# Attention with post-norm, then a 4-bit feed-forward, on one core: residual rows and next tokens loaded three slots sooner; at the seam between the two phases one weight load and two weight stores issued earlier

## The reference

```
qkv   = x @ w_qkv.T                      # 16 heads of 32
attn  = softmax(causal(q k.T / sqrt(32))) v
x1    = layernorm(x + attn @ w_o.T)
gate, up = x1 @ Wg.T, x1 @ Wu.T          # 512 -> 4096, weights as 4-bit codes
out   = layernorm(x1 + (gelu_tanh(gate) * up) @ Wd.T)
```

## Time and profile before

| what | value |
|---|---|
| unprofiled runs, median of 3 | 2737.24 us |
| profiled execution, its own time | 2741.44 us |
| its span, first to last instruction | 2739.6 us |
| TensorE busy | 2644.6 us, 97% of the span |
| VectorE, ScalarE, GpSimd busy | 57%, 40%, 30% |
| mean granted TensorE clock | 0.984 of full |
| moved by DMA | 493.5 MB, 180 GB/s on the mean |

### The profile page before, as it was taken

How to read it: one execution, slowest core, us unless ns; L and a number is a source line. 1 busy time by engine, 2 the same in 40 slices (tenths; PEclk the granted TensorE clock), 3 DMA queues, 4 the chain that set the end, 5 groups by cost and what they waited for, 6 DMA issues and landing times.

```text
span 2739.6 us, 37716 instructions
## 1 busy us (share of the span) xinstructions
PE 2644.6 (97%) x13314; PEld 2156.6 (79%) x13314; DVE 1552.0 (57%) x3224; ACT 1104.4 (40%) x2518; POOL 824.0 (30%) x992
## 2 busy tenths in 40 slices
PE   7999999999888999999999999999999999999998
PEld 6777777777566888888888888888888888888886
DVE  5677677767776888886433333543333364333334
ACT  4666665656543544443222222322222232222221
POOL 1444344434533443443211111321111132111112
PEclk9999999999889999999999999999999999999999
DMA  8676767676547565555554334355434435433441
GB/s 234 156 199 171 200 189 190 156 201 182 146 142 303 196 225 219 197 213 210 200 205 172 139 153 193 139 200 213 163 138 158 188 139 200 187 159 138 162 184 47
DMA packets 143085, 493.52 MB, mean 180 GB/s; under 512 B 11568, under 2 KB 48560, under 8 KB 118320
## 3 DMA queue, kind: packets, MB, share of 16 engines
q1 hardware_dynamic: 142896, 491.11, 52.3%
HBM read 356.84 MB, written 134.22 MB: 179 GB/s over the span
## 4 chain that ended last, share of the span: by engine, by line
PE 69%; DVE 2%; DMA 1%; issue 1%; POOL 0%; ACT 0%; SPq 0%; POOLq 0%; DVEq 0%; ACTq 0%
PE bank L1034 23%; PE bank L1036 23%; PE bank L1035 23%; DMA scale<-gate_scales 1%; PE bank L448 0%; PE bank L434 0%; DMA scale<-up_scales 0%; POOL probs L736 0%; DVE bstats L1482 0%; DVE acc L1425 0%; DMA x1T_scratch<-x_late 0%; DVE bits L1388 0%; PE bank L415 0%; SPq L915 0%; PE bank L458 0%
## 5 line engine op out<-in xcount | busy, mean ns | idle before, releaser
L1643 POOL TENSOR_TENSOR inter_l<-hid,inter_h 128x512 fp32r<-128x512 f32 x256 | 337.3, 1318 | 1375.5 <-ACT inter_h L1165 1375.5
L1425 DVE TENSOR_TENSOR acc<-acc,bank 128x512 f32<-128x512 f32 x512 | 350.0, 685 | 332.7 <-PE bank L1036 323.1
L1034 PE MATMUL bank<-wd,inter_h 128*128 128x512 f32 x1024 | 399.5, 390 | 10.7 <-DVE acc L1425 10.5
L1036 PE MATMUL bank<-wd,inter_l 128*128 128x512 f32 x1024 | 398.9, 390 | 0.0
L1035 PE MATMUL bank<-wd,inter_h 128*128 128x512 f32 x1024 | 398.9, 390 | 0.0
L736 POOL TENSOR_SCALAR probs<-probs,row_inv 128x128 f32<-128x128 f32 (+3 forms) x512 | 264.3, 538 | 363.4 <-DVE row_inv L657 363.4
L1444 DVE TENSOR_TENSOR hid<-hid,bank 128x512 f32<-128x512 f32 x192 | 131.9, 687 | 399.9 <-PE bank L1036 398.3
L1034 PE MATMUL bank<-bx_h,wg 128*128 128x512 f32 x896 | 350.4, 391 | 2.8 <-ACT bank L1165 2.8
L1035 PE MATMUL bank<-bx_l,wg 128*128 128x512 f32 x896 | 349.9, 390 | 0.0
L1036 PE MATMUL bank<-bx_h,wg 128*128 128x512 f32 x896 | 349.6, 390 | 0.0
L1034 PE MATMUL bank<-bx_h,wu 128*128 128x512 f32 x896 | 348.8, 389 | 0.0
(11 more groups left out here) (139 smaller groups left out, 4372.0 us busy)
## 6 DMA issues: line engine op xcount, KB each, us to landing
wg<-w_scratch SPq DMA_DIRECT2D x48, 1792.0 KB, 9.0
wu<-w_scratch SPq DMA_DIRECT2D x48, 1792.0 KB, 12.8
wd<-w_scratch SPq DMA_DIRECT2D x48, 1024.0 KB, 4.9
q_st<-qk_scratch SPq DMA_DIRECT2D x128, 256.0 KB, 5.1
k_st<-qk_scratch SPq DMA_DIRECT2D x128, 256.0 KB, 7.1
w_scratch<-wg SPq DMA_DIRECT2D x16, 1792.0 KB, 9.4
w_scratch<-wu SPq DMA_DIRECT2D x16, 1792.0 KB, 6.4
qk_scratch<-q_stage SPq DMA_DIRECT2D x32, 512.0 KB, 2.8
```

What stands on the lines that cost most here:

```text
L1034: pe.matmul(out, a(0), b(0), start=start, stop=False, skip_group_check=True)
L1036: return pe.matmul(out, a(1), b(0), start=False, stop=stop, skip_group_check=True)
L1425: dve.tensor_tensor(a, a, d_bank[n % 2][:, :], ALU.add).then_inc(d_added, 1)
L1643: pool.tensor_tensor(inter[1][:, m, t, :], hid[:, 2 * m + t, :], f32(inter[0][:, m, t, :]), ALU.subtract).then_inc(inter_split, 1)
```

## The change

In attention, chunks 0 and 1 of the next tokens are issued in slot 2 in place of slot 5. Chunks 2 and 3 stay in slots 6 and 7. The load of the residual rows is issued in slot 1 in place of slot 4; in the drain it stays in slot 0. In both places the load comes behind the slot's q or k write, and in slot 1 behind the stack read.

At the seam, SyncE issues the store of the up tile of round 0 at n = 25, and unit 7 and the store of the down tile at n = 30, which is ahead of the last two transposed tiles and ahead of the wait for attention's last stores. `rest` keeps the second load of `acc`. On VectorE `gate_up_low(1, 1)` moves from n = 28 to n = 29, and `down_low(0)` from n = 28 to n = 30, ahead of `unpack(5)`, which moves from n = 29 to n = 30.

```diff
@@ SyncE, attention @@
-                    if OUT_SLOT <= s + 1 < NEXT_SLOT and nxt:
-                        for c in (0, 1) if s + 1 == OUT_SLOT else (s + 2 - OUT_SLOT,) if s + 2 < NEXT_SLOT else ():
+                    if s in (2, OUT_SLOT, OUT_SLOT + 1) and nxt:
+                        for c in (0, 1) if s == 2 else (s + 2 - OUT_SLOT,):
                             load_x(b + 1, c)
...
-                    if s == (4 if cur else 0) and prev:
+                    if s == (1 if cur else 0) and prev:
@@ SyncE, feed-forward @@
             if n == 25:
                 load_unit(5)
                 store_w(0, 0)
+                store_w(0, 1)
...
+            if n == 30:
+                load_unit(7)
+                store_w(0, 2)
 
         def rest():
-            load_unit(7)
             load_acc(0, 1)
-            store_w(0, 1)
-            store_w(0, 2)
@@ VectorE, feed-forward @@
             if n == 28:
                 times_up(0, 1, 1)
+            if n == 29:
                 gate_up_low(1, 1)
+                times_up(0, 1, 0)
+            if n == 30:
                 down_low(0)
-            if n == 29:
-                times_up(0, 1, 0)
                 unpack(5)
```

## The result

The changed kernel took 2698.53 us (median of 4 runs, 2696.95 to 2699.56) against 2738.2 us for the kernel before (median of 4, 2732.85 to 2740.02). The ratio is 0.9858, 95% interval 0.9841 to 0.9875. The forecast was 2698, range 2687 to 2716. The profiled execution of the changed kernel spans 2695.2 us at a mean granted clock of 0.992, against 2739.6 us at 0.984.

A forecast was written before the change was run, and what follows sets the result against it. TensorE, busy 97% of the span, was taken to set the pace, so only idle or slow-clock time could be won. 27.8 + 4.5 + 7 = 39.3 us off 2737.24 gave 2698 us, range 2687 to 2716.

The forecast's parts named there:

- part 1: Attention, batches 0 to 6: next tokens issued in slot 2 remove the idle time of slot 6; 27.8 us.
- Part 2: Residual rows issued in slot 1, behind the k stack: delay to the stack 0 to 0.3 us, taken as none.
- Part 3: Batch 7: residual rows no longer queued ahead of the feed-forward's first tokens; 4.5 us, from 3 to 6.
- Part 4: Seam: 3.4 MB less ahead of unit 8, 7.9 us, less 1 us of delay; 7 us, bounds 3 to 15.
- It is worth little, since a later release holds TensorE anyway: Seam: removing TensorE's first idle time, 2.52 us before a late transposed tile, by VectorE's new order gains little.
- 3 us later in all: Seam: SyncE's last transposed tiles delayed 3 us, some 2.5 us from four issues, plus the down store ahead.
- Net 1 us later for the queue behind: Seam: the 3 us delay less some 2 us for unit 7's three issues leaves 1 us for later transfers.
- Units 9 and 10 are served by the same queue and move by the same time: Seam: units 9 and 10 land sooner by as much as unit 8, so 7 us was taken.
- A: Rival, slot 4 of batches 1 to 7: k stack lands late by sharing, 21 us back, 2719 us; chance 0.12.
- B: Rival: attention gains, the seam does not, through SyncE's later release or GpSimd's sums; 2705 us; chance 0.15.
- C: Rival: k stack lands only with residual rows and next tokens both, 6.9 us late; slower, 2745 us; chance 0.03.
- D: Rival: the change doesn't reach slot 6, another release lies close behind or slot 2's loads are late; about 2733 us; chance 0.04.

The follow-up runs named there:

- e1: Kernel before with only the next tokens' chunks 0 and 1 moved to slot 2; residual rows and seam as before: 2709.21 us, ratio 0.9898.
- e2: Kernel before with only the residual rows' load moved to slot 1; tokens stay in slot 5, seam as before: 2710.39 us, ratio 0.9904.
- e4: Changed kernel with the residual rows issued in slot 1 directly ahead of the k stack in place of directly behind it: 2720.72 us, ratio 0.9941.
- e5: Kernel before with only VectorE's new order at the seam; SyncE as before: 2734.42 us, ratio 0.9982.
- e9: Changed kernel with unit 7's load and the down tile's store put back behind the two late transposed tiles (n = 31): 2694.34 us, ratio 0.9841.
- e3: Kernel before with only the seam's edits of SyncE and VectorE; attention as before: 2734.58 us, ratio 0.9986.
- e7: Kernel before with only the up tile's store moved to n = 25; all else as before: 2732.87 us, ratio 0.9985.
- e8: Changed kernel with unit 8 loaded at n = 31, ahead of the final waits, and units 9 and 10 ahead of stores: 2693.6 us, ratio 0.9836.
- e10: As e9, with units 8, 9 and 10 each loaded ahead of the weight stores in their way in round 1: 2690.07 us, ratio 0.9826.

## Why the prediction was right, point by point

- **What bounds the kernel, and part 1.** Right. Forecast 27.8 us for batches 0 to 6, measured 28.5, batches 2 to 6 22.5 and 22.4. Pricing the stall by the period rather than by the idle time was what made it so: the idle time alone fell from 22.1 us to 1.6, which is 20.5.
- **What the forecast did not say of parts 1 and 2.** It gave part 1 the whole of the 27.8 us and part 2 nothing but risk and batch 7. By e1 and e2 that split is one of two equally good ones: in batches 1 to 6 the rows' move alone does the same. The sum was not touched by it.
- **Part 2.** Right, with the reason confirmed from both sides: 5.2 us with 1 MB behind, 7.6 us and 14.1 us of waits with it ahead (e4). The Trainium skill ("DMA: Bandwidth & Descriptors", Queues, rings and completion order) says that each DMA engine consumes descriptors in ring order, but that a later one may finish its write before an earlier one. By e4 against the change, the order decided here.
- **Part 3.** Mis-sized: forecast 4.5 us with an upper end of 6, measured 6.4. The wait for the tokens fell by 4.0 us, near the 4.6 forecast, but TensorE's idle time of 4.13 us went together with the slow pace of what follows. The clock was left out of the term here and put into part 1, and it is nearly all of the remaining 2.3 us. In the kernel before, TensorE took 5.01 us from the transposes at 712.79 to the product at 717.80 (granted clock 0.50 from 713 to 717); the same row of products takes 2.93 us in the changed kernel, from 672.21 to 675.14 at a granted clock of 1.00. That is 2.1 us.
- **Part 4.** The size was inside its bounds (3 to 15) but too high: forecast 7, measured 5.4 (mean of three against three), 6.6 in the pair of profiles only with the 1.5 us of luck behind M2. Two steps of it did not hold. "It is worth little, since a later release holds TensorE anyway" failed: e5 is 3.8 us by that edit alone, because SyncE waits for the same copy. And the delay of SyncE was put at "3 us later in all", with the down tile's store mostly passing while the tiles are issued. The tiles were indeed issued 3 us later, where some 2.5 were forecast (49.9 against 46.8 us behind M1; `unpack(5)` ended 1.4 us later and not "where it ended"). But they then took 6.7 us to landing in place of 4.9, and SyncE's wait for them ended 4.9 us later behind M1 (57.5 against 52.5). That is the 5 us which the forecast had as its lower bound. "Net 1 us later for the queue behind" holds for unit 8 (57.9 against 56.7) and not for `acc` (57.5 against 54.6). Against e9 the loss is larger still, since there the tiles leave 6.6 us sooner.
- "Units 9 and 10 are served by the same queue and move by the same time" held for the units: behind M1, unit 8 was in place 6.3 us sooner (65.8 against 72.0), unit 9 5.6 (80.6 against 86.2) and unit 10 5.1 (87.3 against 92.5), and M2 came 5.1 sooner. It did not shorten the idle time there, which went from 2.76 us to 1.65 and 3.22.
- **The Trainium skill's rule on part 4** ("DMA: Bandwidth & Descriptors", same section: a transfer's semaphore write lands only after every earlier write of that DMA engine) would by the prediction's estimate have given 5 us, nearer to the 5.4 measured than the 7 forecast. The late tiles took 6.7 us to landing with the down store ahead of them and 4.9 (before) and 4.6 us (e9) without, 1.8 to 2.1 us, near the 2.4 of that estimate. But plain order of service would make the same difference, and no run here tells the two apart.
- **Rivals.** A did not occur (e4 shows what it would have been). B did not occur as a whole, but half of its reason did: SyncE's new wait, with the store behind it, gave back 3.3 us. C and D did not occur.
- **The signs.** Slot 7, the periods, the stack (5.2 us) and ScalarE's wait for a store came out as forecast; GpSimd's wait fell to 3.62 us, not about 3. The idle time before `add_down(0, 2)` is 5.01 us where 2 to 4 were forecast, the mark of the oversized part 4. SyncE's wait for the late tiles, 5.6 us, stayed below the 6 that would have shown B.
- **The sum.** 39.3 forecast, 40.0 in the profiles without the luck of the pair, 39.7 in the medians. Part 3 was 1.9 too low and part 4 1.6 too high; that the total is right to half a microsecond owes something to that.

## What to carry to other kernels

When two transfers stand in each other's way on one queue, moving either may win nearly all; look for the stretches in which only one of them exists (here the first and the last batch) before adding the two gains. A wait that moves forward in a queue is to be checked against every entry it passes, not for when they leave now but for when they could leave after the rest of the change: here one half of the change had the late tiles ready sooner, and the other half put a wait and a store in front of them. To size a seam, cut the trace between two marks on the bounding engine: medians of runs that spread by 7 to 12 us did not rank the parts, a stretch of 95 us that repeats within 1 us did.

## What the runs showed of the hardware that was not expected

**The clock behind an idle time is not set by its length alone.** In e3 the same 32 value products in slot 7 ran at the full pace behind 3.62 us of idle TensorE and at the slow pace behind 2.31 us. TensorE's timeline in batches 2 and 6, and the same two stretches (the granted clock stands third from the right: 1.00 from 610 us, 0.60 from 243 us):

```profile
243.05 3.89 PE L448 MATMUL bank<-pT,v_rows 128*32 128x512 f32 x32 [2.31 <-ACT pT L512]
...
610.05 2.36 PE L448 MATMUL bank<-pT,v_rows 128*32 128x512 f32 x32 [3.62 <-ACT pT L512]
```

```profile
610.00:613.00 3.00, 2.95 (x38) 1.79 (x39) 0.27 (x2) 0.78 (x4) 2.06 (x4) 1.00 0.54 135
...
243.00:247.00 4.00, 3.95 (x33) 1.52 (x34) 0.27 (x2) 0.79 (x4) 2.06 (x4) 0.60 0.96 185
```

The stretch from 610 us ran at 2.4 GHz throughout, that from 243 us for a good part at 1.2 GHz. The kernels that keep these waits (before, e3, e5 to e7) spread by 7 to 12 us between runs, those without them in attention (the changed kernel, e8 to e10) by 2 to 7, in fewer runs; that the clock makes the difference was not tried by itself.

**An issue itself can stall.** SyncE spent 4.45 us on one weight store, issued 3.8 to 5 us behind three others; in e10, where the loads go first, the stores of that stretch took 0.3 to 0.5 us each. SyncE in the changed kernel:

```profile
794.89 4.45 SPq L938 DMA_DIRECT2D w_scratch<-wg  x1
```

In the kernel before the store at the same place took 7.38 us. That it is the number of stores under way that matters was not tried.
